# Decoder layer on one core: three buffers of the self attention cleared at the start, the fourth and one split of inputs moved behind the masking of the table

## The reference, cut to what matters

```python
q, k, val = (proj(Wq), proj(Wk), proj(Wv))
R_hat = (1.0 + jnp.exp(vv)) / (1.0 + jnp.exp(vv - wv * R))
scores = jax.nn.relu(jnp.einsum('bhqd,bhkd->bhqk', q, k)) * R_hat[None]
scores = jnp.where(causal[None, None], -jnp.inf, scores)
attn = jax.nn.softmax(scores / np.sqrt(hd).astype(x.dtype), axis=-1)
ctx = jnp.einsum('bhqk,bhkd->bhqd', attn, val)
```

## Time and profile before

| | |
|---|---|
| time, median of 3 runs | 2468.52 us (2468.2, 2468.52, 2473.67) |
| the profiled execution's own time | 2468.12 us |
| span in its profile | 2466.3 us |
| PE busy | 2378.6 us, 96% of the span |
| DVE busy | 1540.8 us, 62% |
| ACT busy | 1323.6 us, 54% |
| POOL busy | 1320.3 us, 54% |

### The profile page before, as it was taken

How to read it: one execution, slowest core, us unless ns; L and a number is a source line. 1 busy time by engine, 2 the same in 40 slices (tenths; PEclk the granted TensorE clock), 3 DMA queues, 4 the chain that set the end, 5 groups by cost and what they waited for, 6 DMA issues and landing times.

```text
span 2466.3 us, 58741 instructions
## 1 busy us (share of the span) xinstructions
PE 2378.6 (96%) x21728; PEld 2050.7 (83%) x21728; DVE 1540.8 (62%) x2621; ACT 1323.6 (54%) x3287; POOL 1320.3 (54%) x1130
## 2 busy tenths in 40 slices
PE   7999968999999999999999999999999899999999
PEld 6887847888888888888888888888888698998998
DVE  7666677846666766666766667666676725335342
ACT  4777762116666666666666666666666651221311
POOL 4677563326565665656666566665655533333332
PEclk9999989999999999999999999999999999999999
DMA  6777676625767666666666676666767841101010
GB/s 196 198 224 203 191 201 251 242 104 147 191 187 195 188 183 187 189 191 190 185 189 187 190 192 186 185 188 188 196 187 191 233 149 64 39 26 61 2 39 23
DMA packets 271021, 404.21 MB, mean 164 GB/s; under 512 B 126364, under 2 KB 146332, under 8 KB 270748
## 3 DMA queue, kind: packets, MB, share of 16 engines
q1 hardware_dynamic: 246172, 350.25, 49.0%
q10 hardware_dynamic: 24576, 50.36, 8.1%
HBM read 134.11 MB, written 52.43 MB: 76 GB/s over the span
## 4 chain that ended last, share of the span: by engine, by line
PE 74%; DVE 1%; issue 1%; POOL 1%; ACT 0%; SPq 0%; DMA 0%; ACTq 0%; POOLq 0%; DVEq 0%
PE D_ps_p L68 42%; PE D_ps_s L1800 7%; PE D_ps_p L1826 6%; PE E_ps_g L68 5%; PE E_ps_u L68 5%; PE E_ps_d L68 5%; PE E_ps_y L68 3%; DVE D_columns L1611 0%; PE E_ps_t L1852 0%; SPq L1252 0%; DMA E_w_int<-in_w_gate 0%; ACT D_e L1476 0%; POOL D_e L1360 0%; DVE D_turned L1625 0%; POOL E_acts_low L1409 0%
## 5 line engine op out<-in xcount | busy, mean ns | idle before, releaser
L1360 POOL TENSOR_SCALAR D_e<-D_e,D_columns 128x722 f32<-128x722 f32 x256 | 538.9, 2105 | 528.2 <-DVE D_columns L1617 528.2
L1476 ACT ACTIVATE D_e<-D_ps_s,D_columns 128x723 f32<-128x723 f32 x512 | 438.2, 862 | 408.7 <-DVE D_columns L1611 358.2
L1611 DVE TENSOR_REDUCE D_columns<-D_ps_s 128x1 f32<-128x723 f32 x512 | 439.7, 900 | 303.1 <-PE D_ps_s L1800 302.9
L1625 DVE STREAM_TRANSPOSE D_turned<-D_e 128x768 f32<-128x768 f32 x512 | 496.4, 973 | 5.1 <-DMA D_pT<-D_turned 4.0
L68 PE MATMUL D_ps_p<-D_ctx_high,cross_wk_high 128*128 128x362 f32 (+1 forms) x1024 | 350.0, 342 | 1.5 <-DVEq L1637 1.5
L68 PE MATMUL D_ps_p<-D_ctx_low,cross_wk_high 128*128 128x362 f32 (+1 forms) x1024 | 336.6, 329 | 0.0
L68 PE MATMUL D_ps_p<-D_ctx_high,cross_wk_low 128*128 128x362 f32 (+1 forms) x1024 | 335.0, 327 | 0.0
L68 PE MATMUL D_ps_p<-cross_wv_high,D_ctx_high 128*128 128x512 f32 (+1 forms) x768 | 303.9, 396 | 0.0
L68 PE MATMUL D_ps_p<-cross_wv_high,D_ctx_low 128*128 128x512 f32 (+1 forms) x768 | 303.3, 395 | 0.0
L68 PE MATMUL D_ps_p<-cross_wv_low,D_ctx_high 128*128 128x512 f32 (+1 forms) x768 | 301.8, 393 | 0.0
L1483 ACT ACTIVATE D_e<-D_e,D_columns 128x722 f32<-128x722 f32 x256 | 230.9, 902 | 6.1 <-DVE D_columns L1617 6.1
(11 more groups left out here) (217 smaller groups left out, 5095.9 us busy)
## 6 DMA issues: line engine op xcount, KB each, us to landing
D_pT<-D_turned SPq DMA_DIRECT2D x1536, 96.0 KB, 2.7
D_pT<-D_turned ACTq DMA_DIRECT2D x512, 96.0 KB, 2.8
D_craw<-in_ctxT SPq DMA_DIRECT2D x124, 361.0 KB, 4.0
self_q<-A_q_out SPq DMA_DIRECT2D x10, 640.0 KB, 4.1
self_k<-A_k_out SPq DMA_DIRECT2D x10, 640.0 KB, 3.8
self_v<-A_v_out SPq DMA_DIRECT2D x25, 256.0 KB, 3.6
A_q<-self_q SPq DMA_DIRECT2D x32, 200.0 KB, 3.6
A_k<-self_k SPq DMA_DIRECT2D x32, 200.0 KB, 4.1
```

The lines of the kernel that those rows point to most:

```text
L1360: pool.tensor_scalar(head, head, inv[:, 2 * (s % 2):2 * (s % 2) + 1], None, ALU.mult)\
L1476: act.activation(e[n // 2 % 2][:, n % 2, 0:PARTS * PART].rearrange("p (a c) -> p a c", a=PARTS), parts_of(n), ACT.Exp, bias=neg_max[:, n % ...
L1611: dve.tensor_reduce(neg_max[:, n % 4:n % 4 + 1], parts_of(n), AX.XY, ALU.max, negate=True)\
L1625: dve.transpose(turned[quad % 2][:, :, 2 * (s % 2) + h, :].rearrange("p j (t r) -> p t j r", r=32), e[s % 2][:, h, :].rearrange("p (t j r) ...
```

## The change

Only POOL's program changes, and in it only the order, and one wait goes.

- Both buffers `e` and `pT[1]` are cleared right behind `minus_half`, ahead of the first wait for inputs, where they stood behind the four splits.
- `split_x(1, 3)` is taken from behind `split_x(1, 2)` and put behind the masking of the table.
- The clearing of `pT[0]` goes behind that split. Its wait for `w_low` to reach 12 is dropped; the wait for `rhat_step` in front of the masking comes later in DVE's program than the twelfth `w_low`.

```diff
                 pool.memset(minus_half[:, :], -0.5).then_inc(consts, 1)
+                for tile in e:
+                    pool.memset(tile[:, :, :], 0.0).then_inc(cleared, 1)
+                pool.memset(pT[1][:, :, :, :], 0.0).then_inc(cleared, 1)
                 second = slice(HALF, GT)
...
-                for k in range(KD):
+                for k in range(KD - 1):
                     split_x(1, k)
-                for tile in e:
-                    pool.memset(tile[:, :, :], 0.0).then_inc(cleared, 1)
-                pool.memset(pT[1][:, :, :, :], 0.0).then_inc(cleared, 1)
-                pool.wait_ge(w_low, 3 * KD)
-                pool.memset(pT[0], 0.0).then_inc(cleared, 1)
                 pool.wait_ge(rhat_step, 2 * QUADS + 1)
                 pool.affine_select(out=rhat[:, :, :], in_=rhat[:, :, :], compare_op=ALU.is_ge, fill=-MASK,
                                    base=0, pattern=[[0, H], [-1, T]], channel_multiplier=1).then_inc(rhat_done, 1)
+                split_x(1, KD - 1)
+                pool.memset(pT[0], 0.0).then_inc(cleared, 1)
                 pool.wait_ge(cleared, 4)
```

## The result

The changed kernel takes 2465.73 us in the median of 22 runs (2459.37 to 2472.01); the kernel before, beside it on the same chip, 2473.61 (2467.88 to 2479.41, 22 runs). The ratio is 0.9973, with a 95% interval of 0.9966 to 0.9980: 6.7 us less (4.9 to 8.4), or 0.27%. The ratio lies between the quotients of the two means (0.9974, 6.5 us) and of the two medians (0.9968, 7.9 us); gains are given by the ratio here. The profiled execution took 2464.76 us, with a span of 2463.0; its clock is 0.986 where before had 0.987.

What follows compares the result with a forecast made beforehand. The prediction took the table's chain, held up by POOL's clearings, to set the pace early on. Savings of 0.54 and 5.36 us, taken as 5.9, lead from 2468.12 to 2462.2, plus 0.4 to 2462.6 us; range 2458.5 to 2468.

Steps and rivals of the forecast that it cites:

- What bounds this stretch: First 60 us: the chain that makes the table sets the pace, not PE, and POOL's clearings hold up DVE.
- The sum of 5.9 us: DVE's second table group: L697 saves 0.54 and four L703 save 5.36, taken as 5.9 us.
- Clearings at the start: nothing: Three clearings at 1.99 on POOL, beside DVE's L806: cost taken as 0, upper bound 1.26 us.
- Split and clearing behind the mask: nothing: POOL's 4.1 us beside `scale` and two maxima: cost taken as 0, hidden by 2.1 us of slack.
- The rival that the contention moves along: Split and clearing behind the mask hold up the first `scale` by up to 4.1 us: gain 1.8; chance 0.07.
- PE's hole as the cap: PE's hole ahead of the second scores shrinks from 6.40 to 0.5 us, which caps the gain.
- The clock's gain is not carried: PE from 56.58 to 60.7: 2.1 us saved if the clock's fall goes, not counted, as PE waits for the moves.
- the rival, priced at 2.1 us: PE's first steps: the clock's 2.1 us add up, gain 8.0, time 2460.5; chance 0.17.
- Carried to the end: Behind `scale` nothing the chain needs has a date of its own, so 5.9 us reach the span's end.
- The absolute time: Whole kernel: 2462.2 us for an execution like the profiled one, 2462.6 with the runs' median 0.4 above it.

Runs made afterwards that it cites:

- the other profile of before: The kernel before, unchanged, profiled a second time; first `scale` at 48.34, span less it 2421.0 us.
- one split ahead: Changed kernel with the second and third split behind the mask too, the rest between the first normalisations; ratio to before 0.9969.
- the filled kernel before: The kernel before with 28 matmuls of no use ahead of PE's second scores and 11 behind them; ratio to before 0.9985.
- cleared five times: The kernel before with each of the four buffers cleared five times in the old place; ratio to before 1.0117.
- The two filled kernels: Kernel before (28 and 11) and changed kernel (1 and 14) with useless matmuls ahead of and behind PE's second scores; ratios to before 0.9985 and 0.9987.
- all in that form: The kernel before with the table's multiplications and additions of one on DVE given a second SBUF input; ratio to before 0.9983.
- cleared twice: The kernel before with each of the four buffers cleared twice in the old place; ratio to before 1.0019.
- multiplications with two inputs: The kernel before with the table's sixteen multiplications on DVE as tensor_tensor instead of tensor_scalar; ratio to before 0.9984.
- only behind the mask: Changed kernel with the three clearings back behind the three splits; executed once, 2473.86 us.

## Why the prediction was right, point by point

- **What bounds this stretch.** Right: the table's chain set the pace, and POOL's clearings held it up. Doubling them moved `scale` by 6.99 us, and a form of instruction that does not contend passed them by. Two readings were too strong. The slow instructions are not "exactly those that run while POOL works": L697 took 0.36 us three times in before and not twice, once of them at 24.62 with POOL at work. And the wait was not for one instruction of POOL: it lasted from 34.68 to 40.46, past the starts of three more clearings, the last two at 36.83 and 38.58. The rule named there is borne out in that the later one waits fully; how many of POOL's instructions it waits for, the two profiles of before answer differently.
- **The sum of 5.9 us.** Right in each term: L697 0.55 (0.54 predicted), L703 5.36 (5.36), `scale` 5.95 earlier. The match to 0.05 us is in part luck. It was one of two cases, and the profiled execution of the changed kernel fell in the same one as that of before: in the other profile of before the clearings cost the group 3.3 us, and `scale` was 2.0 us earlier. Against that one the change brings 3.8 to 4.2 us.
- **Clearings at the start: nothing.** Right, and the rule beside it too: L806 took 1.70 us beside them.
- **Split and clearing behind the mask: nothing.** Right: `scale` 1.82, the two maxima behind it 1.88 as before, slack 2.24 us. The rival that the contention moves along is out.
- **PE's hole as the cap.** Right in its size (0.48 left), but it was no cap for the table's chain: with one split ahead, `scale` moved on by 1.1 to 1.5 us, and PE's hole behind the second scores shrank from 3.32 to 2.57.
- **The clock's gain is not carried.** Not settled. The prediction thought that the fall may not come; it came, 3.4 us long. That the moves pace the first weighted sum is borne out: it started 21.8 us behind `scale` with the clock at 1.00, as without. That nothing is therefore gained at the end is not: the filled kernel before gained 3.7 us (1.2 to 5.9), and for the rival, priced at 2.1 us, there is that number; against it, the changed kernel gained nothing by filling.
- **Carried to the end.** Borne out in the profiles. The span less `scale` is 2416.0 to 2426.7, with a mean of 2420.1; a straight line through the fourteen profiles gives 1.03 us of span for each us of `scale`, with a standard error of 0.12 (without the run cleared five times 0.93 and 0.24). Five times the clearing cost 28.9 us in the median. So a shift of the first `scale` is carried about as a whole, with a scatter from 4 us below to 7 us above. This is why the two profiled spans differ by only 3.3 us while the medians differ by 7.9. The two filled kernels, which do not differ, speak against it.
- **The absolute time.** The predicted 2462.6 is 3.1 below the measured median, though the gain was 5.9 against 6.7. The step at fault is the base, "the median of the runs shown lies 0.4 above that execution": 22 runs put it 5.5 above. The predicted ratio, 2462.6 / 2468.52 = 0.9976, lies inside the interval.

What stays open. That `scale` comes earlier because the clearings and the split no longer hold up the table is shown; that the whole gain at the end comes from there is not. The measured gains (6.7 and 6.9 us, intervals 4.9 to 8.4 and 4.0 to 9.6) are somewhat over the 4 to 6 that `scale` shows. The scatter behind `scale` can hold the difference. It has no single place: from the first to the last `scale` the profiles have 290.4 to 298.5 us, behind it 2123.4 to 2128.5, and the 5.0 us between the two profiles of before lie wholly behind the last one (2123.5 and 2128.5). The kernel with the multiplications in two-input form gained 4.0 us (1.5 to 6.7) with `scale` only 0.6 earlier in its profile, and the one with all in that form 4.2 (1.2 to 6.9) with `scale` 3.4 earlier. These two are level although their `scale` differs by 2.8, which their intervals still allow; the two filled kernels are level at 6.35, which the estimate above does not allow. An untested rival is that the changed kernel gains in part by PE's shorter idleness in the first steps, which filling gives to both; what behind `scale` makes the differences is not settled.

## What to carry to other kernels

When one instruction of a group is twenty times its median, lay the other engine's timeline beside it and look what ends where it ends: work that "nobody waits for" on POOL can hold up DVE with no semaphore between them, and no view of waits names it. Ask of each fill or copy on POOL which DVE instructions run beside it and in what form, and put it where DVE runs reciprocals, reductions or nothing; taking the contention from one instruction is worth little (0.58 us here) if the next one behind it has the form that waits. For changes below 0.3%, take the base from many runs. Read what the change did at the event that moved, and what it is worth from many runs of both; the two ends of two profiles give neither.

## What was not expected of the hardware

- The same program has two courses. In the profiles where POOL's copy of the first split (L478, near 21.4) took 3.0 to 3.3 us, DVE waited for a whole run of clearings (before, cleared twice, multiplications with two inputs, only behind the mask, before with its holes filled: up to 13.18 us for four multiplications). Where it took 0.7 us and the subtraction behind it 3.85, DVE got in between clearings (before again at each of their ends, cleared five times at each but the first). Seven of seven profiles. Clearings followed each other every 1.75 us, and about every 1.86 where DVE got in between; in the run cleared five times the distance was 1.75 again once DVE was done, so it goes with getting in and does not foretell it. What sets which course it is was not tried. One row of before, then two of before again:

```profile
21.49 3.19 POOL L478 CAST A_x_high<-A_xraw 128x640 fp32r<-128x640 f32 x1 [6.36 <-DMA A_xraw<-in_xT]
```
```profile
21.45 0.74 POOL L478 CAST A_x_high<-A_xraw 128x640 fp32r<-128x640 f32 x1 [6.21 <-DMA A_xraw<-in_xT]
22.28 3.85 POOL L480 TENSOR_TENSOR A_x_low<-A_xraw,A_x_high 128x640 fp32r<-128x640 f32 x1
```

- A record that waits can overlap its follower: in the run only behind the mask the four L703 of the first group show 8.67 us from 27.59, to 36.26, while L697 starts at 30.95. Durations of waiting instructions are then not to be added.
- Filling PE's idle time did not remove the fall of its clock: one came at the next wait (0.47 us matmuls from 73.9 on), where the unfilled kernel had 0.31 us.
- The words on the kernel before say that the only ordering between engines is by semaphores. Here DVE waited 5.4 us for POOL's clearings, and no semaphore of the kernel asked for it.
